# First pages split whole, and the scale bounds reduced across partitions on GpSimd, in an attention and FFN block

## The chip, the cores and the metric
The kernel runs on one core of a Trainium2 chip. The core has five engines with an instruction list each: TensorE (PE, matrix products), ScalarE (ACT), VectorE (DVE), GpSimd (POOL) and SyncE (SP, here the issuer of nearly all DMAs). Engines wait for one another through semaphores. The metric is the device time of one execution in microseconds (us), the median of several runs.

## The reference
One transformer layer on x of shape 4 x 512 x 1024, in float32:

```python
x = layernorm(x + attention(x))     # 32 query heads, 8 key/value heads of 32, rotary, causal softmax, @ wo
gate_w, up_w, down_w = gate_t * gate_s[:, None], up_t * up_s[:, None], down_t * down_s[:, None]
hidden = silu(x @ gate_w.T) * (x @ up_w.T)      # 3584 wide, weights are -1, 0 or 1 times a scale
x = layernorm(x + hidden @ down_w.T)
```

## The kernel before
All matrix operands are float16. Where one float16 is not exact enough, a tensor is kept as two parts: "hi", its rounding, made by ACT, and "lo", what is left, made by DVE. A product of two such tensors is three matmuls. The weights of the FFN are whole numbers and need one part; their scales are applied later.

The program has two stages that overlap a little. Attention goes through 16 units (8 heads of one batch each, about 46 us). For every unit PE computes projections ("proj": q, and for a new batch kv), scores by query row ("score_q", only for the row maxima that DVE takes), scores by key ("score_k"), the values times the exponentials ("pv", line 1027) and sums of the exponentials ("sums"). ACT makes the exponentials, POOL masks the diagonal block of each ("causal", line 1510), and POOL adds exponentials of two key tiles ("presum", line 1518) so that PE's sums are shorter. A projection result is rotated by DVE ("rotate", lines 1295 to 1297), added up by POOL ("rope_add", line 1504), split by ACT and DVE ("nat_hi", "nat_lo") and turned by a transposing DMA ("stack"). The FFN is a Strassen-like scheme on PE over two passes.

Nobody writes the order of instructions out. Each piece of work is `put` into a plan with an engine, a rank (a due time), a duration and the pieces that it comes after. `Plan.close` simulates the engines: of the pieces that may start, each engine takes the one with the lowest rank. The result is one list for each engine, which the hardware then executes in that order. The ranks are in slots of 46 us. A DMA's share of the queue is given as `moves`. So a changed duration, rank or dependency can reorder every engine's list.

The first twelve pages (512 KB each: x tiles, wq and wkv weights; `FIRST`, line 68) are loaded by SP at once and split in the order of loading ("split_hi" on ACT, lines 1143 and 1145; "split_lo" on DVE, lines 1271 and 1275). The first three are split in two halves (`HALVED = 3`), and PE's first products wait for half a page only.

The FFN needs a bound of the hidden values: the largest gate scale times the largest up scale, over all partitions. DVE reduces the two scale tensors (128 x 28) along the free axis, which leaves 128 x 2 numbers ("bound", 0). SP stores these to DRAM and loads all 256 of them back into every partition, in the buffer row0, and DVE reduces again (line 1403) and derives the scales that ACT's silu and DVE use in the FFN ("bound", 1). The first load of a row of x into row0 waits for it.

Of the kernel before, what the change touches and what calls it, by code (L numbers as in the profile page):

```python
# [17 lines left out]
KD = D // P  # L18
# [40 lines left out]
SLOT = 46.0  # L59
HOP = .15  # L60
LANDS = 1.9
FIRST_MOVES, PAGE_MOVES, FORM_MOVES, TURN_MOVES, FORMS_MOVE = 1.3, 1.85, .95, 1.31, 3.3
# [7 lines left out]

HALVED = 3
# [132 lines left out]
class Plan:  # L204
# [69 lines left out]
def attention_plan(plan):  # L274
# [6 lines left out]
    ranks = {w: -200.0 + n if n < NFIRST - 4 else SLOT * (-1.6 + .1 * (n - NFIRST + 4)) for n, w in enumerate(FIRST)}  # L281
# [10 lines left out]
    for n, (what, b, j) in enumerate(loads):  # L292
        at = ranks[what, b, j]
        before = n - 2 if n >= NFIRST + 2 else NFIRST - 1 if what == "wo" else -1
        last = [loads[n - 1]] if n else []
        put(SY, at, .4, "page_load", what, b, j, moves=2 * FIRST_MOVES if n == 0 else FIRST_MOVES if n < NFIRST else PAGE_MOVES,
            after=[("split_lo", *loads[before])] if before >= 0 else [])
        put(SC, at, 1.04, "split_hi", what, b, j, after=[("page_load", what, b, j)] + [("split_hi", *w) for w in last] + (
            [("proj", "q", UNITS * b - 1, j, KD - 1)] if what == "x" and b else []))
        put(VE, at, 1.25, "split_lo", what, b, j, after=[("split_hi", what, b, j)] + [("split_lo", *w) for w in last])  # L300
# [125 lines left out]
def output_done(plan, tile, end):  # L426
# [4 lines left out]
    row += [("bound", 1)] if tile == 0 else []  # L431
# [210 lines left out]
def block_kernel(nc, xT, x, wq, wkv, wo, gateT, upT, downT, gate_s, up_s, down_s,  # L642
                 rope, causal, identH, identB, out):
    bound_dram = nc.dram_tensor("scale_bounds_spill", [P, 2], F32, kind="Internal").ap()
# [8 lines left out]
    plan.put(SY, SLOT, .4, "bound_store", moves=.1, after=[("bound", 0)])  # L653
    plan.put(SY, SLOT + 3, .4, "bound_load", moves=.3, after=[("bound_store",)])
    plan.put(VE, SLOT + 6, 1.6, "bound", 1, after=[("bound_load",)])
# [5 lines left out]
    with ctx:  # L661
        def sem(name):
            return ctx.enter_context(nc.semaphore(name))
# [79 lines left out]
        s_half_hi, s_half_lo = sem("first_half_hi"), sem("first_half_lo")  # L743
# [25 lines left out]
        s_bound_out, s_bound_in = sem("bound_store_dma"), sem("bound_load_dma")  # L769
# [157 lines left out]
        def tensor_program(e):  # L927
# [12 lines left out]
            for kind, which in plan.order[PE]:  # L940
                if kind == "proj":
# [8 lines left out]
                    if what == "out":  # L950
                        if k == 0:
                            late = att_late(w)
                            on.wait_ge(s_att_in[late], 16 * len([t for t in range(w + 1) if att_late(t) == late]))
                        on.wait_ge(s_lo, split_n["wo", 0, k] + 1)
                        dst, cols = bank[n % 2][:, :], slice(part * HALF, (part + 1) * HALF)
                        left, right = att[att_late(w)], wo_p
                        rows = slice(0, P)
                    elif what == "q":
                        b, g = divmod(w, UNITS)
                        n_x, n_w = split_n["x", b, part], split_n["wq", g, k // 4]  # L960
                        if n_x < HALVED and k < KD // 2:
                            on.wait_ge(s_half_lo, n_x + 1)
                        else:
                            on.wait_ge(s_lo, n_x + 1)
                        if n_w < HALVED and k % 4 < 2:
                            on.wait_ge(s_half_lo, n_w + 1)
                        else:
                            on.wait_ge(s_lo, n_w + 1)
                        dst, cols = bank[n % 2][:, 0:UH * HD], slice(g * UH * HD, (g + 1) * UH * HD)
                        left, right = xT_p, wq_p  # L970
                    else:
                        on.wait_ge(s_lo, split_n["x", w, part] + 1)
                        on.wait_ge(s_lo, split_n["wkv", 0, k // 2] + 1)
                        dst, cols = bank[n % 2][:, :], slice(0, 2 * NKV * HD)
                        left, right = xT_p, wkv_p
# [144 lines left out]
        def scalar_program(e):  # L1120
            on = Waits(e)
            e.dma_start(tab[:, :, :, :], rope).then_inc(s_tab, 16)
            for kind, which in plan.order[SC]:
                if kind == "split_hi":
# [128 lines left out]
        def vector_program(e):  # L1253
# [7 lines left out]
            for kind, which in plan.order[VE]:  # L1261
                if kind == "split_lo":
# [4 lines left out]
                    up, whole = X_UP if which[0] == "x" else W_UP, as_parts(which[0], src)  # L1267
                    if n < HALVED:
                        mid = hi.shape[1] // 2
                        on.wait_ge(s_half_hi, n + 1)  # L1270
# [124 lines left out]
                elif kind == "bound":  # L1395
                    if which[0] == 0:
# [96 lines left out]
        def gpsimd_program(e):  # L1493
# [4 lines left out]
            for kind, which in plan.order[PO]:  # L1498
# [20 lines left out]
                elif kind == "newton":  # L1519
# [8 lines left out]
                    nc.gpsimd.tensor_scalar(w, mv[:, n % 2, 0:1], r, -1.0, ALU.mult, ALU.mult).then_inc(s_newton, 1)  # L1528
                elif kind == "scale_row":
# [41 lines left out]
        def sync_program(e):  # L1571
            on = Waits(e)
            for kind, which in plan.order[SY]:
# [42 lines left out]
                elif kind == "bound_store":  # L1616
                    on.wait_ge(s_bound, 1)
                    e.dma_start(bound_dram, sc[:, 0:2]).then_inc(s_bound_out, 16)
                elif kind == "bound_load":
                    on.wait_ge(s_bound_out, 16)  # L1620
                    e.dma_start(row[0][:, 0:2 * P], bound_dram.rearrange("a c -> (a c)").partition_broadcast(P)).then_inc(s_bound_in, 16)
# [154 lines left out]
```

## Time and profile before
| | |
|---|---|
| median of 3 runs | 1853.55 us (1852.56 to 1855.95) |
| profiled execution | 1853.55 us, its span 1851.8 us |
| PE | busy 1802.5 us, 97% of the span |
| DVE | 1188.8 us, 64% |
| ACT | 709.7 us, 38% |
| POOL | 533.6 us, 29% |

The span is the time from the first to the last instruction in the trace; the execution's own time lies a little above it. A busy share is an average over the whole span: in the first 130 us DVE is the more loaded engine beside PE, later PE is busy almost without a break. A wait of PE is put down to the instruction that released it. Instructions that load code, issue DMAs or handle semaphores do not count as busy and have no row in a timeline of busy work; they can only be seen as idle time.

### The profile page before, as it was taken

Reading aid. Unit: us, or ns where it says so; the run is one execution under the profiler, and the core shown is the slowest. Engines: PE = TensorE matmul, PEld = TensorE weight load, DVE = VectorE, ACT = ScalarE, POOL = GpSimd, SP = SyncE. Lnnn points to the kernel's source line nnn. Section 1 sums busy time; section 2 is a strip of 40 time slices with the busy share of each in tenths; the row PEclk is TensorE's granted clock in tenths of the full one; section 3 lists DMA queues with packets and bytes.
Section 4 is the critical chain, followed back from the end, with each engine's and each line's share of the span. In section 5 each row is a group of like instructions: output and inputs, shape, how many; then the busy total and the mean of one; then the engine's idle time right before and its main releaser. Section 6 shows DMA issues by size and latency. Waiting matters only on the chain.

```text
span 1851.8 us, 27052 instructions
## 1 busy us (share of the span) xinstructions
PE 1802.5 (97%) x10384; PEld 873.7 (47%) x10384; DVE 1188.8 (64%) x2063; ACT 709.7 (38%) x1115; POOL 533.6 (29%) x805
## 2 busy tenths in 40 slices
PE   8989999999999999999999999999999999999998
PEld 5645555555555533444444444444444444444444
DVE  7996778678767763555545444745656765667646
ACT  5444435344434444346433343341232322222221
POOL 2454546446546554221000000211311211122203
PEclk9999999999999998999999999999999999999999
DMA  8453334225324397567743353549311221222301
GB/s 257 103 146 55 70 92 130 60 70 144 78 49 115 92 225 214 187 223 261 249 169 131 109 196 136 213 145 211 128 66 54 73 73 42 81 95 86 118 12 80
DMA packets 228592, 233.24 MB, mean 126 GB/s; under 512 B 184048, under 2 KB 184432, under 8 KB 228464
## 3 DMA queue, kind: packets, MB, share of 16 engines
q1 hardware_dynamic: 227600, 231.13, 42.3%
q8 instruction: 82, 1.34, 0.3%
q10 hardware_dynamic: 864, 0.39, 0.1%
q14 instruction: 46, 0.38, 0.1%
HBM read 122.68 MB, written 72.88 MB: 106 GB/s over the span
## 4 chain that ended last, share of the span: by engine, by line
PE 88%; DVE 5%; issue 2%; SPq 2%; DMA 1%; ACT 1%; POOL 1%; DVEq 0%; ACTq 0%
PE bank L1082 32%; PE bank L978 21%; PE bank L1102 13%; PE bank L1115 6%; PE bank L1027 4%; PE bank L990 4%; PE bank L1014 3%; PE bank L1042 3%; PE bank L993 1%; DVE down_forms L1453 1%; SPq L1654 1%; DVE gate_blocks L1447 1%; DVE up_blocks L1437 0%; DVE down_forms L1430 0%; DVE xT_parts L1275 0%
## 5 line engine op out<-in xcount | busy, mean ns | idle before, releaser
L1082 PE MATMUL bank<-x_forms,weight_forms 128*128 128x512 f16 x3136 | 700.5, 379 | 11.7 <-DVE up_blocks L1437 3.7
L1082 PEld LDWEIGHTS bank<-x_forms,weight_forms 128*128 128x128 f16 x3136 | 305.4, 98 | 385.5 <-issue 7.1
L1174 ACT ACTIVATE p_tiles<-bank 128x512 f32<-128x512 f32 (+1 forms) x352 | 193.0, 557 | 291.9 <-PE bank L1014 290.2
L1310 DVE TENSOR_REDUCE row_max<-bank 128x1 f32<-128x384 f32 (+3 forms) x352 | 219.9, 636 | 90.8 <-PE bank L993 89.7
L1102 PE MATMUL bank<-down_forms 128*128 128x512 f16 (+1 forms) x1168 | 258.1, 376 | 2.4 <-issue 2.4
L978 PE MATMUL bank<-wq_parts,xT_parts 128*128 128x256 f16 x1536 | 216.8, 274 | 7.9 <-DVE wq_parts L1271 7.9
L1472 DVE TENSOR_TENSOR acc<-bank,acc 128x512 f32<-128x512 f32 x188 | 127.7, 687 | 123.6 <-PE bank L1102 64.7
L1510 POOL TENSOR_SCALAR_AFFINE_SELECT p_tiles<-p_tiles 128x128 f32<-128x128 f32 (+2 forms) x352 | 137.8, 398 | 219.7 <-ACT p_tiles L1174 218.4
L1102 PEld LDWEIGHTS bank<-down_forms 128*128 128x128 f16 x1168 | 114.2, 98 | 137.3 <-issue 2.9
L978 PE MATMUL bank<-wo_parts,att_parts 128*128 128x512 f16 x672 | 171.7, 384 | 1.9 <-DMA att_parts<-att_spill 1.9
L978 PEld LDWEIGHTS bank<-wq_parts,xT_parts 128*128 128x128 f16 x1536 | 144.5, 98 | 59.2 <-issue 12.5
L1534 POOL TENSOR_TENSOR acc<-acc,down_forms 128x1024 f32<-128x1024 f32 x16 | 38.8, 2429 | 375.0 <-DVE acc L1472 375.0
L1115 PE MATMUL bank<-down_forms 128*128 128x512 f16 x560 | 133.6, 379 | 1.7 <-DVE down_forms L1453 1.7
L990 PE MATMUL bank<-k_stack,q_stack 96*128 96x512 f16 (+3 forms) x512 | 126.7, 301 | 4.9 <-DVE row_max L1310 4.7
L1014 PE MATMUL bank<-q_stack,k_stack 98*128 98x512 f16 (+1 forms) x352 | 126.1, 363 | 4.4 <-ACT p_tiles L1174 2.7
L1518 POOL TENSOR_TENSOR p_tiles<-p_tiles 128x512 f32<-128x512 f32 (+1 forms) x62 | 117.2, 1890 | 42.3 <-PE bank L1027 41.8
L1437 DVE TENSOR_TENSOR up_blocks<-bank,up_blocks 128x512 f32<-128x512 f32 x84 | 58.0, 690 | 107.9 <-PE bank L1082 55.9
L1251 ACT ACTIVATE down_forms<-gate_blocks 128x512 f16<-128x512 f32 x102 | 64.0, 628 | 133.1 <-DVE gate_blocks L1447 127.1
L1437 DVE TENSOR_TENSOR gate_blocks<-bank,gate_blocks 128x512 f32<-128x512 f32 x84 | 57.7, 688 | 77.1 <-PE bank L1082 67.5
L1524 POOL TENSOR_SCALAR rstd<-rstd 128x1 f32<-128x1 f32 x93 | 35.3, 380 | 223.3 <-DVE rstd L1374 217.1
L1239 ACT ACTIVATE gate_blocks<-gate_blocks,gate_scale 128x512 f32<-128x512 f32 x84 | 60.5, 720 | 99.1 <-DVE gate_blocks L1437 99.0
L978 PEld LDWEIGHTS bank<-wo_parts,att_parts 128*128 128x128 f16 x672 | 61.6, 98 | 77.5 <-issue 17.9
(121 smaller groups left out, 2049.3 us busy)
## 6 DMA issues: line engine op xcount, KB each, us to landing
weight_forms_spill<-weight_forms SPq DMA_DIRECT2D x28, 896.0 KB, 5.3
weight_forms<-weight_forms_spill SPq DMA_DIRECT2D x28, 896.0 KB, 4.5
x_forms_spill<-x_parts SPq DMA_DIRECT2D x56, 256.0 KB, 2.3
w_page<-gateT SPq DMA_DIRECT2D x28, 512.0 KB, 5.1
w_page<-upT SPq DMA_DIRECT2D x28, 512.0 KB, 4.0
w_page<-downT SPq DMA_DIRECT2D x28, 512.0 KB, 4.1
att_spill<-att_made SPq DMA_DIRECT2D x64, 128.0 KB, 2.2
down_forms<-x_spill SPq DMA_DIRECT2D x16, 512.0 KB, 3.3
```

The costliest lines, as they stand in the source:

```text
L978: t = nc.tensor.matmul(dst, left[:, a, k, rows], right[:, c, k, cols], start=k == 0 and m == 0, stop=last)
L990: nc.tensor.matmul(to[:, h, :], qT[0:STK, u % QS, h0 + h, i * P:n], kT[0:STK, b % 2, kv_of(u, h0 + h), 0:n], start=h == 0, stop=False, ski ...
L1014: nc.tensor.matmul(to, kT[0:STKM, b % 2, (u % UNITS) * UG + G, lo:lo + P], qT[0:STKM, u % QS, heads, lo:S], start=True, stop=True).then_in ...
L1082: t = nc.tensor.matmul(strassen[bank_set(use)][to][:, :], w_form[:, use % 4, A_FORMS[a_form], k * P:(k + 1) * P], xF[:, :, B_FORMS[b_form] ...
L1102: t = nc.tensor.matmul(to[:, 0:cols.stop - cols.start], hid_p[place_of(r)][:, k, a, i // 2 * P:(i // 2 + 1) * P], wd_p[place_of(r)][:, c, ...
L1115: t = nc.tensor.matmul(to[:, :], hid_f[r % NF % 3][:, HID_FORMS.index(a_form), a, pair * P:(pair + 1) * P], wd_f[r % NF % 3][:, DOWN_B[b_f ...
L1174: nc.scalar.activation(p32[j][:, h0:h0 + heads, :], bank[5 + m % 2][:, 0:heads * n].rearrange("p (h c) -> p h c", c=n), ACT.Exp, scale=SCO ...
L1310: nc.vector.tensor_reduce(mx[:, u % 2, i, h0:h0 + ROW_HEADS[i]], bank[3 + m % 2][:, 0:ROW_HEADS[i] * n].rearrange("p (h c) -> p h c", c=n) ...
L1437: nc.vector.tensor_tensor(block, strassen[bank_set(use)]["Z" if k == 1 else "P"][:, :], block, ALU.add).then_inc(s_blk, 1)
L1472: nc.vector.tensor_tensor(dst, got[:, :], dst, ALU.add).then_inc(s_acc, 1)
L1510: nc.gpsimd.affine_select(out=block, in_=block, compare_op=ALU.is_ge, fill=0.0, base=0, pattern=[[0, KEY_HEADS[j]], [1, P]], channel_multi ...
L1518: nc.gpsimd.tensor_tensor(to, to, p32[j + 1][:, :, :], ALU.add).then_inc(s_pre, 1)
```

## The change
Three edits. The first three pages are no longer split in halves: one ACT and one DVE instruction for each page, and PE waits for whole pages. The plan's numbers for the first pages change: the last four of `FIRST` get the same early ranks as the others (before they were due 1.6 to 1.3 slots ahead of time 0), and each takes `PAGE_MOVES` of the queue. The bounds of the scales no longer go through DRAM: POOL runs a `partition_all_reduce` over 128 x 2 numbers, which leaves the maxima in every partition.

```diff
-FIRST_MOVES, PAGE_MOVES, FORM_MOVES, TURN_MOVES, FORMS_MOVE = 1.3, 1.85, .95, 1.31, 3.3
+PAGE_MOVES, FORM_MOVES, TURN_MOVES, FORMS_MOVE = 1.85, .95, 1.31, 3.3
-HALVED = 3
-    ranks = {w: -200.0 + n if n < NFIRST - 4 else SLOT * (-1.6 + .1 * (n - NFIRST + 4)) for n, w in enumerate(FIRST)}
+    ranks = {w: -200.0 + n for n, w in enumerate(FIRST)}
-        put(SY, at, .4, "page_load", what, b, j, moves=2 * FIRST_MOVES if n == 0 else FIRST_MOVES if n < NFIRST else PAGE_MOVES,
+        put(SY, at, .4, "page_load", what, b, j, moves=PAGE_MOVES,
-    row += [("bound", 1)] if tile == 0 else []
-    plan.put(SY, SLOT, .4, "bound_store", moves=.1, after=[("bound", 0)])
-    plan.put(SY, SLOT + 3, .4, "bound_load", moves=.3, after=[("bound_store",)])
-    plan.put(VE, SLOT + 6, 1.6, "bound", 1, after=[("bound_load",)])
+    plan.put(PO, SLOT, 3.0, "bound", 0, 0, after=[("bound", 0)])
+    plan.put(VE, SLOT, .8, "bound", 1, after=[("bound", 0, 0)])
...
-                        if n_x < HALVED and k < KD // 2:
-                            on.wait_ge(s_half_lo, n_x + 1)
-                        else:
-                            on.wait_ge(s_lo, n_x + 1)
...
+                        on.wait_ge(s_lo, split_n["x", b, part] + 1)
+                        on.wait_ge(s_lo, split_n["wq", g, k // 4] + 1)
...
-                    if n < HALVED:
-                        mid = hi.shape[1] // 2
-                        nc.scalar.activation(hi[:, 0:mid], whole[:, 0:mid], ACT.Copy, scale=up).then_inc(s_half_hi, 1)
...
-                        nc.vector.scalar_tensor_tensor(lo[:, 0:mid], whole[:, 0:mid], up, hi[:, 0:mid],
-                                                       ALU.mult, ALU.subtract).then_inc(s_half_lo, 1)
...
-                    on.wait_ge(s_bound_in, 16)
-                    nc.vector.tensor_reduce(sc[:, 2:4], row[0][:, 0:2 * P].rearrange("p (a c) -> p c a", c=2),
-                                            mybir.AxisListType.X, ALU.max).then_inc(s_bound, 1)
...
+                elif kind == "bound":
+                    on.wait_ge(s_set, 2)
+                    on.wait_ge(s_bound, 1)
+                    nc.gpsimd.partition_all_reduce(sc[:, 2:4], sc[:, 0:2], P, bass.bass_isa.ReduceOp.max).then_inc(s_bound, 1)
+                    on.wait_ge(s_bound, 2)
```

DVE's list at the start of the program. L1271 and L1275 are split_lo before (L1249 in the changed file), L1295 to L1297 the rotate (L1270 to L1272), L1304 nat_lo (L1279). Before:

```order
L1275 SCALAR_TENSOR_TENSOR xT_parts<-p_tiles,xT_parts 128x8x128
L1275 SCALAR_TENSOR_TENSOR wkv_parts<-p_tiles,wkv_parts 128x1024
L1295 TENSOR_TENSOR rope_cos<-bank,rope_tab 128x256
L1296 TENSOR_TENSOR rope_sin<-bank,rope_tab 128x8x16
L1297 TENSOR_TENSOR rope_sin<-bank,rope_tab 128x8x16
L1275 SCALAR_TENSOR_TENSOR wkv_parts<-wo_parts,wkv_parts 128x1024 x3
L1304 TENSOR_TENSOR stack_rows<-rope_cos,stack_rows 128x8x32
L1295 TENSOR_TENSOR rope_cos<-bank,rope_tab 128x256
```

Now:

```order
L1249 SCALAR_TENSOR_TENSOR xT_parts<-p_tiles,xT_parts 128x8x128
L1270 TENSOR_TENSOR rope_cos<-bank,rope_tab 128x256
L1271 TENSOR_TENSOR rope_sin<-bank,rope_tab 128x8x16
L1272 TENSOR_TENSOR rope_sin<-bank,rope_tab 128x8x16
L1249 SCALAR_TENSOR_TENSOR wkv_parts<-p_tiles,wkv_parts 128x1024
L1249 SCALAR_TENSOR_TENSOR wkv_parts<-wo_parts,wkv_parts 128x1024
L1279 TENSOR_TENSOR stack_rows<-rope_cos,stack_rows 128x8x32
L1270 TENSOR_TENSOR rope_cos<-bank,rope_tab 128x256
L1271 TENSOR_TENSOR rope_sin<-bank,rope_tab 128x8x16
L1272 TENSOR_TENSOR rope_sin<-bank,rope_tab 128x8x16
L1249 SCALAR_TENSOR_TENSOR wkv_parts<-wo_parts,wkv_parts 128x1024 x2
```

The first rotate has moved ahead of all four wkv pages, and nat_lo with the second rotate ahead of the last two.

POOL's list in the second group of the first unit (about 79 us in the trace). AFFINE_SELECT is causal, the TENSOR_TENSOR on p_tiles is presum, the one on rope_cos is rope_add. Before:

```order
L1510 AFFINE_SELECT p_tiles<-p_tiles 128x512
L1510 AFFINE_SELECT p_tiles<-p_tiles 128x2x128 x2
L1510 AFFINE_SELECT p_tiles<-p_tiles 128x128 x4
L1518 TENSOR_TENSOR p_tiles<-p_tiles 128x4x128
L1510 AFFINE_SELECT p_tiles<-p_tiles 128x128
L1518 TENSOR_TENSOR p_tiles<-p_tiles 128x4x256
L1504 TENSOR_TENSOR rope_cos<-rope_cos,rope_sin 128x256
L1510 AFFINE_SELECT p_tiles<-p_tiles 128x128 x3
```

Now:

```order
L1482 AFFINE_SELECT p_tiles<-p_tiles 128x512
L1482 AFFINE_SELECT p_tiles<-p_tiles 128x2x128 x2
L1504 ISA
L1504 ISA scale_bounds<-scale_bounds 128x2
L1482 AFFINE_SELECT p_tiles<-p_tiles 128x128 x5
L1490 ISA
L1490 TENSOR_TENSOR p_tiles<-p_tiles 128x4x128
L1490 TENSOR_TENSOR p_tiles<-p_tiles 128x4x256
L1476 TENSOR_TENSOR rope_cos<-rope_cos,rope_sin 128x256
L1482 AFFINE_SELECT p_tiles<-p_tiles 128x128 x3
```

The all-reduce stands behind the first three masks of the group, with an ISA instruction that has no tile ahead of it; another such instruction stands ahead of the first presum. One mask has moved ahead of that presum. Such an instruction without a tile also stands ahead of POOL's first rope_add in both kernels.

## Rows read from the trace of the kernel before

**Rows 1.** The page, the chain that ended last, shares of the span by engine.
```profile
PE 88%; DVE 5%; issue 2%; SPq 2%; DMA 1%; ACT 1%; POOL 1%; DVEq 0%; ACTq 0%
```

**Rows 2.** PE's waits, whole span: instruction, releaser, us in total, times, longest us.
```profile
PE bank L978 <- DVE wq_parts L1271: 7.9, 1, 7.9
...
PE bank L1027 <- POOL p_tiles L1510: 3.3, 3, 2.5
```

**Rows 3.** Timeline of ACT, first 10 us: start us, us, instruction, idle before and releaser.
```profile
1.23 1.28 ACT L1143 ACT_TABLE_LOAD   x1 [1.23 <-PEq L1770]
5.11 0.63 ACT L1143 ACTIVATE xT_parts<-p_tiles 128x512 f16<-128x512 f32 x1 [2.60 <-DMA p_tiles<-xT]
...
6.34 0.63 ACT L1143 ACTIVATE wq_parts<-p_tiles 128x512 f16<-128x512 f32 x1
...
8.90 1.06 ACT L1145 ACTIVATE xT_parts<-p_tiles 128x1024 f16<-128x1024 f32 x1
```

**Rows 4.** Timeline of DVE, 10 to 18 us.
```profile
10.06 1.23 DVE L1275 SCALAR_TENSOR_TENSOR xT_parts<-p_tiles,xT_parts 128x1024 f16<-128x1024 f32 x1 [0.41 <-ACT xT_parts L1145]
...
12.89 0.42 DVE L1295 TENSOR_TENSOR rope_cos<-bank,rope_tab 128x256 f32<-128x256 f32 x1 [0.33 <-PE bank L978]
...
13.62 4.02 DVE L1275 SCALAR_TENSOR_TENSOR wkv_parts<-wo_parts,wkv_parts 128x1024 f16<-128x1024 f32 x3
```

**Rows 5.** Timeline of PE, first 26 us.
```profile
7.91 7.56 PE L978 MATMUL bank<-wq_parts,xT_parts 128*128 128x256 f16 x48 [7.91 <-DVE wq_parts L1271]
15.31 10.52 PE L978 MATMUL bank<-wkv_parts,xT_parts 128*128 128x512 f16 x48
```

**Rows 6.** Timeline of POOL, 78 to 92 us.
```profile
78.67 1.54 POOL L1510 TENSOR_SCALAR_AFFINE_SELECT p_tiles<-p_tiles 128x512 f32<-128x512 f32 x3
82.06 0.68 POOL L1510 TENSOR_SCALAR_AFFINE_SELECT p_tiles<-p_tiles 128x128 f32<-128x128 f32 x2 [1.84 <-ACT p_tiles L1174]
83.77 0.67 POOL L1510 TENSOR_SCALAR_AFFINE_SELECT p_tiles<-p_tiles 128x128 f32<-128x128 f32 x2 [1.03 <-ACT p_tiles L1174]
85.65 1.54 POOL L1518 TENSOR_TENSOR p_tiles<-p_tiles 128x512 f32<-128x512 f32 x1 [1.21 <-PE bank L1027]
...
87.42 2.35 POOL L1518 TENSOR_TENSOR p_tiles<-p_tiles 128x1024 f32<-128x1024 f32 x1
89.73 0.71 POOL L1504 TENSOR_TENSOR rope_cos<-rope_cos,rope_sin 128x256 f32<-128x256 f32 x1
90.41 0.79 POOL L1510 TENSOR_SCALAR_AFFINE_SELECT p_tiles<-p_tiles 128x128 f32<-128x128 f32 x3
```

**Rows 7.** Timeline of PE, 84 to 94 us, the two values groups.
```profile
85.84 0.85 PE L1027 MATMUL bank<-p_tiles,v 128*32 128x384 f32 x8
...
92.98 1.07 PE L1027 MATMUL bank<-p_tiles,v 128*32 128x512 f32 x8
```

**Rows 8.** Timeline of POOL, its first tensor operation and the idle before it.
```profile
13.79 1.63 POOL L1504 TENSOR_TENSOR rope_cos<-rope_cos,rope_sin 128x256 f32<-128x256 f32 x1 [12.29 <-DVE rope_sin L1297]
```

**Rows 9.** DMA issues: issuing engine, operation, count, size, us from issue to landing.
```profile
row<-scale_bounds_spill SPq DMA_DIRECT2D x1, 128.0 KB, 4.8
...
scale_bounds_spill<-scale_bounds SPq DMA_DIRECT2D x1, 1.0 KB, 3.7
```

**Rows 10.** Windows: us, busy of PE, PEld, DVE, ACT, POOL, granted clock, DMA share, GB/s.
```profile
80.00:90.00 10.00, 9.92 (x93) 5.74 (x85) 9.41 (x16) 5.38 (x10) 5.74 (x9) 1.00 0.78 139
100.00:130.00 30.00, 25.42 (x225) 14.18 (x224) 27.61 (x49) 16.62 (x28) 19.61 (x26) 1.00 0.63 151
222.00:227.30 5.30, 3.47 (x21) 1.14 (x21) 4.81 (x8) 3.87 (x7) 4.78 (x8) 1.00 0.57 148
227.30:230.90 3.60, 3.58 (x11) 1.44 (x12) 1.94 (x3) 0.60 (x1) 1.12 (x3) 0.53 0.38 73
```

**Rows 11.** Timeline of PE, 110 to 131 us, the longest wait.
```profile
129.16 0.39 PE L1001 MATMUL bank<-idH,max_parts 128*16 128x128 f16 x4 [2.21 <-DVE max_parts L1320]
```

**Rows 12.** The page, costliest groups, POOL's small operation: busy us, mean ns, idle before.
```profile
L1524 POOL TENSOR_SCALAR rstd<-rstd 128x1 f32<-128x1 f32 x93 | 35.3, 380 | 223.3 <-DVE rstd L1374 217.1
```

More of the change, by code:

```diff
@@ L643, in block_kernel @@
                  rope, causal, identH, identB, out):
-    bound_dram = nc.dram_tensor("scale_bounds_spill", [P, 2], F32, kind="Internal").ap()
     x1_dram = nc.dram_tensor("x1_spill", [TILES, P, D], F32, kind="Internal").ap()
@@ L742, in block_kernel @@
         s_hi, s_lo = sem("split_hi"), sem("split_lo")
-        s_half_hi, s_half_lo = sem("first_half_hi"), sem("first_half_lo")
         s_proj, s_proj_taken, s_v = sem("projected"), sem("projection_taken"), sem("v_copied")
@@ L768, in block_kernel @@
         s_hhi, s_hlo, s_down, s_acc = sem("hid_hi"), sem("hid_lo"), sem("down"), sem("acc")
-        s_bound_out, s_bound_in = sem("bound_store_dma"), sem("bound_load_dma")
         s_bound, s_ds, s_ds_in, s_xrow, s_scaled, s_added = (
@@ L959, in tensor_program @@
                         b, g = divmod(w, UNITS)
-                        n_x, n_w = split_n["x", b, part], split_n["wq", g, k // 4]
-                        if n_x < HALVED and k < KD // 2:
-                            on.wait_ge(s_half_lo, n_x + 1)
-                        else:
-                            on.wait_ge(s_lo, n_x + 1)
[L965 to L968, printed above, removed]
+                        on.wait_ge(s_lo, split_n["x", b, part] + 1)
+                        on.wait_ge(s_lo, split_n["wq", g, k // 4] + 1)
                         dst, cols = bank[n % 2][:, 0:UH * HD], slice(g * UH * HD, (g + 1) * UH * HD)
@@ L1138, in scalar_program @@
                         on.wait_ge(s_proj, proj_n["q", which[1] * UNITS - 1, which[2]] + 1)
-                    up = X_UP if which[0] == "x" else W_UP
-                    hi, whole = parts_of(*which)[0], as_parts(which[0], src)
-                    if n < HALVED:
-                        mid = hi.shape[1] // 2
-                        nc.scalar.activation(hi[:, 0:mid], whole[:, 0:mid], ACT.Copy, scale=up).then_inc(s_half_hi, 1)
-                        hi, whole = hi[:, mid:], whole[:, mid:]
-                    nc.scalar.activation(hi, whole, ACT.Copy, scale=up).then_inc(s_hi, 1)
+                    nc.scalar.activation(parts_of(*which)[0], as_parts(which[0], src), ACT.Copy,
+                                         scale=X_UP if which[0] == "x" else W_UP).then_inc(s_hi, 1)
                 elif kind == "v_copy":
@@ L1266, in vector_program @@
                     on.wait_ge(arrived, 16 * times)
[L1267 to L1270, printed above, removed]
-                        nc.vector.scalar_tensor_tensor(lo[:, 0:mid], whole[:, 0:mid], up, hi[:, 0:mid],
-                                                       ALU.mult, ALU.subtract).then_inc(s_half_lo, 1)
-                        hi, lo, whole = hi[:, mid:], lo[:, mid:], whole[:, mid:]
                     on.wait_ge(s_hi, n + 1)
-                    nc.vector.scalar_tensor_tensor(lo, whole, up, hi, ALU.mult, ALU.subtract).then_inc(s_lo, 1)
+                    nc.vector.scalar_tensor_tensor(lo, as_parts(which[0], src), X_UP if which[0] == "x" else W_UP, hi,
+                                                   ALU.mult, ALU.subtract).then_inc(s_lo, 1)
                 elif kind == "rotate":
@@ L1615, in sync_program @@
                                 att_dram[b, t].rearrange("p a k c -> p (a k c)")).then_inc(s_att_in[att_late(tile)], 16)
[L1616 to L1621, printed above, removed]
                 elif kind == "row_load":
                     tile = which[0]
-                    if tile == 0:
-                        on.wait_ge(s_bound, 2)
                     if tile >= TILES - 2:
```

## The prediction, made before the changed kernel ran

> **What bounds the kernel now.** I read the page first, then the waits of TensorE (PE), then timelines of the stretches that the change touches. The chain that ended last lies on PE for 88% [rows 1], and PE is busy for 97% of the 1851.8 us span: what is off PE matters only where it makes PE wait. PE's waits are few: 7.9 us before its first matmul, 3.3 us in all for GpSimd's (POOL) masked tiles [rows 2]. PE executes its list in order, so one late instruction holds all behind it, and nothing later in the kernel has an idle reserve in which a delay of many microseconds could vanish. The question is what the change does to PE's waits in two places: the first 20 us, and around 80 us.
>
> The profiled execution took 1853.55 us, 1.75 us more than its span; it is also the median of the three runs, so the sum is made on it.
>
> **Part 1, the undivided first pages.** Before, x tile 0 and two wq pages are split in halves. ScalarE (ACT) begins at 5.11, when x lands, and thanks to the halves PE begins at 7.91 [rows 3, 5]. Whole pages cost 1.06 us on ACT and 1.23 us on VectorE (DVE) [rows 3, 4]. x: 5.11 + 1.06 = 6.17 on ACT, then 1.23 on DVE, 7.5 with the hand-over. wq: ACT 6.34 (its landing) + 1.06 = 7.40, DVE 7.5 + 1.22 = 8.7. PE starts at about 8.75: +0.8 us. The three instructions fewer on ACT and on DVE are already in these times.
>
> The new order changes DVE too: the first group's "rotate" moves ahead of the first wkv page, "nat_lo" and the second "rotate" ahead of the last two. The first rotate then starts at 12.89 + 0.8 = 13.7 [rows 4], though DVE was free from 11.3. Then 0.8 for the rotate, 2.5 for wkv pages 0 and 1 (17.0), 0.4 for nat_lo, 0.7 for the second rotate (18.1); wkv page 2, at 1.34 as in the run of three in 4.02 us [rows 4], is done at 19.4 to 19.8. PE begins the wkv group at 15.31 + 0.8 = 16.1 and needs page 2 after 12 of 48 matmuls, 2.6 us later (10.52 us for 48 [rows 5]), at 18.7. It waits 0.7 to 1.1 us; with the pages behind I take 1.2. The start costs +2.0 us; bounds 0.8 (only the first) and 3.
>
> **Part 2, the bounds of the scales.** Removed: a store and its broadcast load, 3.7 and 4.8 us from issue to landing [rows 9], two issues on SyncE's queue, a small reduction on DVE, and the wait of the first row load. All of this lay beside PE's work, and its result is first needed in the FFN, hundreds of microseconds later: I cost the removal at nothing; at most DVE's reduction, under half a microsecond, comes back.
>
> Added on POOL: the all-reduce and, as the order shows, an instruction without a tile just before it and one just before the next TENSOR_TENSOR. I read these two as changes of POOL's loaded code; the only other one stands, in both kernels, ahead of the first rope_add. The plan books 3.0 us for the all-reduce and nothing for the loads. The trace hides the price of the one in before: POOL sat idle 12.29 us there and was ready when DVE released it [rows 8], so it takes at most 12.29 us. From below, the nearest row is ACT's table load, 1.28 us [rows 3]. The middle is 6.8, and a small transfer out to memory and back takes 3.7 + 4.8 = 8.5 us [rows 9]. I take 7 us for each. The all-reduce of 128x2 is bounded by POOL's small operation, 0.38 us [rows 12], and by the round trip that it replaces, 8.5 us; with two elements to a partition I take 1 us, near the small row.
>
> The Trainium skill has a price for this load (GPSIMD Engine Reference, section 2.1, Instruction dispatch): the first call after a load pays about 6 us, with no visible instruction in the profile. No row here shows it. With 6 for 7, twice, the sum would be 2 us less, 1863.9; by this rule the change makes two such calls, and it speaks against the change.
>
> Now the queue. Before, POOL ends three masks at 78.67 + 1.54 = 80.21 and is idle for 1.84 us [rows 6]. There stand now the load and the all-reduce: 80.2 + 7 + 1 = 88.2. Behind them four masks (0.68 + 0.67), done at 89.4 with a hand-over less. PE's group at 85.84 [rows 7] waits for the fourth: it starts at 89.4, a stall of 3.5 us. ACT and DVE run dry with it, since their banks come from PE. On POOL one more mask (89.7), the second load (96.7), the two sums 1.54 and 2.35 (100.5), rope_add 0.71 and three masks 0.79 (102.0) [rows 6]. PE's 128x512 group, begun at 92.98 before [rows 7], needs them: it starts at 102.0. In all +9.0 us, the second stall being 5.5. Of the 15 us added to POOL, its idle takes the rest: 1.84 and 1.21 us [rows 6], 1.8 between 90.41 + 0.79 = 91.2 and 92.98, and the waits between masks.
>
> **Given back.** From 100 to 130 DVE is busy 27.6 of 30 us [rows 10], and PE waits 2.21 us for it at 129 [rows 11]. While PE stalls DVE catches up, so a part goes: I take 1.2 (bounds 0 and 3, should the smaller waits go as well).
>
> **The clock.** From 222 to 227.3 PE was busy 3.47 of 5.3 us, and in the 3.6 us after it the granted clock was 0.53, so nearly all at the lower level of 1.2 GHz [rows 10]: about 1.7 us lost. Both stalls are longer than that idle time; but from 100 to 130 single waits of up to 2.21 us left the clock at 1.00 [rows 10, 11]. I take 1.7 for the second stall, 0.8 for the first: +2.5 (bounds 0 and 5).
>
> Sum: 2.0 + 9.0 - 1.2 + 2.5 = +12.3; 1853.55 + 12.3 = 1865.9 us.
>
> **Rivals.**
> A, not slower: the loads hide. If load and all-reduce fit in the idle 1.84 us and the second load in the 3 us of 1.21 + 1.8, POOL's new work is covered, and DVE's slack around 129 pays the start's 2.0 back. It decides at a load of about 1.5 us, near the 1.28 of [rows 3]. The time is 1853.55 + 2.0 - 1.2 = 1854.4, with the start at 0.8 and 2.2 back 1852.2. Against it: every transfer from memory cited here took 3.7 us or more.
> A half way: the second load does nothing, because the code is still there. Then the first stall alone remains: 1853.55 + 2.0 + 3.5 - 1.2 + 0.8 = 1858.7.
> B, slow loads: the DMA queues move 139 GB/s from 80 to 90 us [rows 10], and a load that shares them takes 10 us to the upper bound of 12.3. Each load's excess over 7 adds to PE's delay in full: at 12.3 it is 9.0 + 5.3 + 5.3 = 19.6, the clock 3.4, and the time 1853.55 + 2.0 + 19.6 - 1.2 + 3.4 = 1877.4.
> C, a slow all-reduce, 8.5 us: +7.5, 1873.4. Past about 11 us for load and all-reduce together DVE, whose own step of the bounds waits for it, holds back row maxima too.
> For A speaks that POOL's load is invisible before; for B that the nearest row, [rows 8], would allow it; for C that nothing across partitions runs on POOL before.
>
> **How the numbers follow.** Forecast (loads of 5 to 9 us) 0.60; A 0.11; the single load 0.08; B 0.12; C 0.06; faster by a way I have not priced, DVE's catching up above all, 0.03. A difference of 0.2%, 3.7 us, is what a measurement of this kernel can tell from none. Slower: 0.60 + 0.08 + 0.12 + 0.06 less 0.01 for a single load that costs little, 0.85; the same: A and that 0.01, 0.12; faster 0.03. The forecast's own range is 1860 (loads of 5, clock at 1) to 1872 (loads of 9, clock at 5). For 8 in 10 I go down to 1857, which holds the single load, and up to 1875, which holds C and the milder half of B.
>
> **What would show it.** Right: the first matmul near 8.7 us; PE waiting about 1 us for wkv parts; on POOL a gap of about 7 us ahead of the all-reduce and again ahead of the next 128x512 sum, with no row of work in it; PE's longest waits at its values groups for POOL, 3 to 4 and 5 to 6 us; the granted clock below 1 behind the second. Wrong: PE waiting under 2 us for POOL between 80 and 110 (then the loads were mispriced, A); the gaps there but the span grown much less (given back later, to be seen in DVE's share after 100 us); no wait for wkv parts (DVE's new order was covered).

## The result, and the profile after

The changed kernel takes 1865.6 us (median of 4 runs, 1864.1 to 1866.4) beside 1853.05 us (4 runs, 1849.9 to 1856.0) for the kernel before: a ratio of 1.0067, 95% interval 1.0049 to 1.0086. It is slower, by 12.6 us; forecast were 1865.9 us. (The later comparisons timed the kernel before again, 13 to 27 runs each, with medians of 1854.1 to 1855.3 us; beside these the difference is 10.3 to 11.5 us.) The profiled execution took 1864.6 us with a span of 1862.9, 11.05 us more than that of before, and the points below are set against these 11.05 us.

The chain that ended last lies on TensorE (PE) for 87% (88% in [rows 1]): PE is still the bound. PE's waits, over the whole span (instruction, releaser, us in total, times, longest), answer to [rows 2]:
```profile
PE bank L964 <- DVE wq_parts L1249: 8.9, 1, 8.9
PE bank L1013 <- POOL p_tiles L1482: 8.3, 4, 2.7
...
PE bank L964 <- DVE wkv_parts L1249: 0.9, 2, 0.7
```
The first matmul comes 1.0 us later, there is a new wait for wkv parts, and the waits for GpSimd (POOL) went from 3.3 to 8.3 us. PE's start, beside [rows 5]:
```profile
8.87 7.04 PE L964 MATMUL bank<-wq_parts,xT_parts 128*128 128x256 f16 x48 [8.87 <-DVE wq_parts L1249]
15.74 2.75 PE L964 MATMUL bank<-wkv_parts,xT_parts 128*128 128x512 f16 x12
19.19 1.47 PE L964 MATMUL bank<-wkv_parts,xT_parts 128*128 128x512 f16 x6 [0.70 <-DVE wkv_parts L1249]
```
VectorE (DVE) at the same time, beside [rows 4]: the first rotate's product stands ahead of every wkv page, after 1.95 us of idle time, and the next rotate ahead of the last two pages.
```profile
10.15 1.22 DVE L1249 SCALAR_TENSOR_TENSOR xT_parts<-p_tiles,xT_parts 128x1024 f16<-128x1024 f32 x1
13.32 0.42 DVE L1270 TENSOR_TENSOR rope_cos<-bank,rope_tab 128x256 f32<-128x256 f32 x1 [1.95 <-PE bank L964]
...
17.93 2.88 DVE L1249 SCALAR_TENSOR_TENSOR wkv_parts<-wo_parts,wkv_parts 128x1024 f16<-128x1024 f32 x2
```
POOL's timeline from 78 us, beside [rows 6]. Both gaps are "issue": POOL waited for nothing that the profile shows. The instructions without a tile have no row here, but the view of a line lists them, as MODIFY_POOL_CONFIG (POOL's configuration instruction): at 83.0 us ahead of the all-reduce and at 91.6 us ahead of the sum. Each gap begins there.
```profile
80.53 2.53 POOL L1482 TENSOR_SCALAR_AFFINE_SELECT p_tiles<-p_tiles 128x512 f32<-128x512 f32 x3
89.77 0.48 POOL L1504 PARTITION_ALL_REDUCE scale_bounds<-scale_bounds  x1 [6.71 <-issue]
90.33 1.28 POOL L1482 TENSOR_SCALAR_AFFINE_SELECT p_tiles<-p_tiles 128x128 f32<-128x128 f32 x5
98.31 3.74 POOL L1490 TENSOR_TENSOR p_tiles<-p_tiles 128x512 f32<-128x512 f32 x2 [6.70 <-issue]
102.01 0.72 POOL L1476 TENSOR_TENSOR rope_cos<-rope_cos,rope_sin 128x256 f32<-128x256 f32 x1
102.68 0.79 POOL L1482 TENSOR_SCALAR_AFFINE_SELECT p_tiles<-p_tiles 128x128 f32<-128x128 f32 x3
```
PE's two values groups, beside [rows 7]; they began at 85.84 and 92.98 before. These two waits are 5.4 of the 8.3 us:
```profile
91.42 1.50 PE L1013 MATMUL bank<-p_tiles,v 128*32 128x384 f32 x8 [2.73 <-POOL p_tiles L1482]
...
103.53 1.11 PE L1013 MATMUL bank<-p_tiles,v 128*32 128x512 f32 x8 [2.69 <-POOL p_tiles L1482]
```
Windows, with columns as in [rows 10]; the granted clock is the third number from the end:
```profile
90.80:97.60 6.80, 6.18 (x29) 2.95 (x30) 2.29 (x7) 1.79 (x3) 0.81 (x4) 0.50 0.20 42
97.60:104.30 6.70, 4.01 (x37) 2.65 (x39) 2.56 (x5) 0.63 (x1) 5.02 (x6) 1.00 0.02 4
104.40:107.80 3.40, 3.40 (x22) 0.82 (x15) 2.20 (x10) 0.00 (x0) 0.72 (x1) 0.50 0.40 77
...
1797.00:1801.00 4.00, 3.16 (x8) 1.15 (x9) 0.69 (x1) 0.02 (x1) 0.00 (x0) 0.57 0.00 0
```
The clock stood at its lower level (1.2 GHz, 0.50 of full) behind each of the two stalls. Near 1797 us it fell once more, which it did not in the same window of the kernel before:
```profile
1797.00:1801.00 4.00, 4.00 (x21) 1.78 (x19) 3.10 (x7) 0.00 (x0) 2.27 (x6) 1.00 0.00 0
```

Both kernels have 10,384 matmuls. Counting them in the order of their starts and taking one trace from the other gives PE's delay at any time of before. It is what the steps below are measured by: 2.8 us at 78 us; 5.6 at the first values group and 10.55 at the second; 10.1 from 154 to 1200 us; 9.6 at 1340; 11.05 at 1840. How far chance goes in it the launches with the same first pages show, at 78 us: -0.3, -0.4, 0.6 and 0.0 us with those of before (e1, e5, e6, e9), 2.8, 2.8 and 4.0 us with those of the change (the changed kernel, e2, e3).

### The profile page after: what moved, and what is told of

Read it like the earlier page. It is cut to its first block, busy times and chain, and to the rows that moved or that the text cites. A ratio compares the mean times of both kernels' runs of the same rounds, so it can differ in the third digit from the quotient of the medians.

```text
span 1862.9 us, 27050 instructions
## 1 busy us (share of the span) xinstructions
PE 1808.5 (97%) x10384; PEld 875.0 (47%) x10384; DVE 1187.1 (64%) x2059; ACT 709.8 (38%) x1112; POOL 529.4 (28%) x806
## 4 chain that ended last, share of the span: by engine, by line
PE 87%; DVE 6%; issue 2%; SPq 2%; DMA 1%; POOL 1%; ACT 1%; DVEq 0%; ACTq 0%; POOLq 0%
PE bank L1068 32%; PE bank L964 20%; PE bank L1088 13%; PE bank L1101 6%; PE bank L1013 4%; PE bank L976 3%; PE bank L1000 3%; PE bank L1028 2%; PE bank L979 1%; DVE down_forms L1425 1%; SPq L1623 1%; DVE gate_blocks L1419 1%; DVE row_max L1285 0%; DVE up_blocks L1409 0%; DVE down_forms L1402 0%
## 5 line engine op out<-in xcount | busy, mean ns | idle before, releaser
L1068 PE MATMUL bank<-x_forms,weight_forms 128*128 128x512 f16 x3136 | 700.4, 379 | 11.1 <-DVE up_blocks L1409 3.7
L1013 PE MATMUL bank<-p_tiles,v 128*32 128x128 f32 (+3 forms) x1024 | 95.0, 451 | 8.4 <-POOL p_tiles L1482 8.3
L964 PE MATMUL bank<-wkv_parts,xT_parts 128*128 128x512 f16 x384 | 97.8, 379 | 0.9 <-DVE wkv_parts L1249 0.9
```

The costliest lines, as they stand in the source:

```text
L964: t = nc.tensor.matmul(dst, left[:, a, k, rows], right[:, c, k, cols], start=k == 0 and m == 0, stop=last)
L1013: t = nc.tensor.matmul(bank[PV_BANK[q]][h * HD:(h + 1) * HD, lo:S], value, p32[j][:, h, :], start=j == NT - 1, stop=j == 0, tile_position= ...
L1068: t = nc.tensor.matmul(strassen[bank_set(use)][to][:, :], w_form[:, use % 4, A_FORMS[a_form], k * P:(k + 1) * P], xF[:, :, B_FORMS[b_form] ...
```

## The experiments

The times of before in these comparisons are medians of 1854 to 1855 us (13 to 27 runs). One launch's trace carries chance of its own: stretches at the low clock near 227 and 1790 us come and go between launches and those near 700 us vary in length, a shorter one being worth about 1.7 us. So the ratios decide between kernels, and the traces show places.

**e1: the all-reduce alone.** The kernel before in all its orders and pages; only the bounds go through POOL.
```diff
+    plan.order[SY] = [p for p in plan.order[SY] if p[0] not in ("bound_store", "bound_load")]
+    plan.order[PO].insert(plan.order[PO].index(("causal", (0, 1, 2, 2))) + 1, ("bound", (0, 0)))
```


> The kernel before, with its own lists on every engine, in which alone the DRAM round trip of the bounds is taken out and the all-reduce stands on POOL behind the third mask of the second group. My theory: two gaps of 6.7 us on POOL, PE 3 us late behind the first and 8.1 us late behind the second, of which DVE's slack gives back at most 2; with about 1.5 us for a lower clock the time is 1853 + 8 = 1860 to 1862 us. Rival (the reordering of the lists is the larger part of the +11 us): 1853 to 1856.

Measured: 1863.97 us, ratio 1.0047 (1.0032 to 1.0062). POOL, and what PE waited for from 78 to 130 us:
```profile
85.46 0.55 POOL L1529 PARTITION_ALL_REDUCE scale_bounds<-scale_bounds  x1 [5.54 <-ACT p_tiles L1174]
86.08 1.05 POOL L1507 TENSOR_SCALAR_AFFINE_SELECT p_tiles<-p_tiles 128x128 f32<-128x128 f32 x4
93.92 1.25 POOL L1515 TENSOR_TENSOR p_tiles<-p_tiles 128x512 f32<-128x512 f32 x1 [6.80 <-issue]
```
```profile
PE bank L1027 <- POOL p_tiles L1507: 7.5, 3, 5.6
```
PE's delay goes from -0.3 us at 78 to 8.3 at 111. Most of the loss is here, with the start untouched. The view puts the first gap, 5.54 us, down to ACT's exponentials; but the all-reduce reads only scale_bounds, and its MODIFY_POOL_CONFIG stands at 79.9 us, where the gap begins. I take it for the load, shorter than the 6.71 us above. The time lies above the 1860 to 1862 us that I had expected; the trace has two low-clock stretches that its kernel before has not, near 138 and 1797 us.

**e2: the start alone.** Whole pages and the new ranks, the bounds by the round trip.
```diff
-HALVED = 3
+HALVED = 0
-    ranks = {w: ... else SLOT * (-1.6 + .1 * (n - NFIRST + 4)) ...}
+    ranks = {w: ... else -200.0 + n ...}
-        put(SY, at, .4, "page_load", ..., moves=2 * FIRST_MOVES if n == 0 else ...,
+        put(SY, at, .4, "page_load", ..., moves=PAGE_MOVES,
```


> The changed kernel's first pages and plan numbers alone; the bounds go through DRAM as before. My theory: the first matmul near 8.8 us, PE 2.7 to 2.9 us late from 35 to 95 us, and about 1 us late from 180 us on, since DVE's slack gives the rest back: 1853 + 1 = 1854 us, within noise. Rival (the start's delay stays to the end): 1856.

Measured: 1853.99 us, ratio 0.9995 (0.9984 to 1.0007). PE is 2.8 us late at 78 us and 0.5 at 154: the start's delay is given back almost whole.

**e3: a second all-reduce behind the first**, in the changed kernel. It tells the price of the operation from the price of what stands ahead of it.
```diff
+                    nc.gpsimd.partition_all_reduce(sc[:, 6:8], sc[:, 0:2], P, ...ReduceOp.max)
```


> The changed kernel with a second all-reduce of the same numbers directly behind the first, into two unused columns. My theory (the 6.7 us ahead of the all-reduce is the change of POOL's code): the second begins without such a gap, costs 0.5 us, and the time is 1865 to 1867 us. Rival (the gap is the launch of an all-reduce): another gap of 6.7 us, and the time is 1871 to 1873 us.

Measured: 1866.5 us (one run). POOL:
```profile
90.92 0.54 POOL L1505 PARTITION_ALL_REDUCE scale_bounds<-scale_bounds  x1 [6.64 <-issue]
91.57 0.35 POOL L1507 PARTITION_ALL_REDUCE scale_bounds<-scale_bounds  x1
92.00 1.28 POOL L1483 TENSOR_SCALAR_AFFINE_SELECT p_tiles<-p_tiles 128x128 f32<-128x128 f32 x5
100.76 3.73 POOL L1491 TENSOR_TENSOR p_tiles<-p_tiles 128x512 f32<-128x512 f32 x2 [7.48 <-issue]
```
The second one costs 0.35 us and has no gap. The gap belongs to the exchange of POOL's code, not to the all-reduce. The five masked selects run straight behind an all-reduce; the way back is paid by the next TENSOR_TENSOR.

**e4: the all-reduce first on POOL.** The scales are loaded first and DVE forms their maximum first; the hope was that POOL's 12.3 idle us [rows 8] hide everything.
```diff
+    plan.order[PO].insert(0, ("bound", (0, 0)))
+    plan.order[VE].insert(0, ("bound", (0,)))
```


> As the first kernel, but the scales are loaded at the start of the program, DVE reduces them first, and POOL's all-reduce stands ahead of its first rope_add, where POOL was idle for 12.29 us. My theory: the loads of code fall into that idle, the first rope_add comes 1 to 2 us later at 15.4, PE does not notice, and the time is that of before, 1852 to 1854 us. Rival (the loads cost PE their time wherever they stand, or the loads collide with the first pages): 1858 or more.

Measured: 1862.47 us, ratio 1.0038 (1.0023 to 1.0053). My expectation was wrong and the rival right:
```profile
12.74 0.69 POOL L1530 PARTITION_ALL_REDUCE scale_bounds<-scale_bounds  x1 [11.25 <-issue]
23.57 0.71 POOL L1502 TENSOR_TENSOR rope_cos<-rope_cos,rope_sin 128x256 f32<-128x256 f32 x1 [10.14 <-issue]
```
```profile
PE bank L980 <- DVE rope_sin L1298: 5.0, 1, 5.0
```
```profile
2.00:12.00 10.00, 3.70 (x18) 2.61 (x19) 5.13 (x10) 6.84 (x9) 0.00 (x0) 1.00 0.99 383
13.00:23.00 10.00, 8.24 (x51) 4.81 (x49) 4.42 (x7) 2.28 (x3) 0.43 (x1) 1.00 0.84 336
23.00:30.00 7.00, 3.75 (x9) 1.34 (x10) 4.60 (x8) 5.69 (x8) 2.35 (x2) 0.53 0.27 54
```
DVE had the maxima only at 6.35 us, 6.4 us before the all-reduce, and its MODIFY_POOL_CONFIG stands at 1.7 us, ahead of the wait for them. If the load ran from there it took 11.0 us, if only once the maxima were ready, 6.4 us; no run tells which. The second gap is 10.14 us, and the rotate that it held up had been ready for 9.3 us, so this load took 9.3 to 10.1 us. This load ran while DMA moved 336 GB/s. The rope sum came at 23.57 instead of 13.79, DVE and then PE waited, and the clock fell.

**e5: the all-reduce where POOL is idle.** Before, POOL has nothing to do from 229.5 to 242.45 us, and DMA moves nothing from 230 to 240 us.
```diff
+    plan.order[PO].insert(plan.order[PO].index(("causal", (4, 1, 2, 2))) + 1, ("bound", (0, 0)))
+    plan.order[VE].remove(("bound", (1,)))
+    plan.order[VE].insert(plan.order[VE].index(("row_max", (5, 3, 5))) + 1, ("bound", (1,)))
```


> The kernel before, with the DRAM round trip replaced by the all-reduce, placed on POOL in the 12.9 us that POOL is idle from 229.5 us on (before its masked select of unit 4 at 242.45), and DVE's second step of the bounds behind it in the idle 1.7 us at 243. No DMA transfer runs from 230 to 240 us in the kernel before. Theory (the cost is what POOL's loads put in front of PE, and a load takes 6.7 us when DMA is quiet): load 6.7 + all-reduce 0.5 + load 6.7 = 13.9 us, ends at 243.4, 1 us after the next select was due; PE at most 1 us later: 1852 to 1856 us, ratio 0.999 to 1.001. Rival (the code load costs wherever it stands, or takes 10 us or more, as it did at the start): 20 us from 229.5, PE stalls 6 us or more: 1860 to 1865. A second rival, that leaving out the round trip brings something in itself: below 1850.

Measured: 1860.88 us, ratio 1.0041 (1.0028 to 1.0055). The theory's number was wrong. POOL, one window, and PE's next values group:
```profile
234.93 0.37 POOL L1531 PARTITION_ALL_REDUCE scale_bounds<-scale_bounds  x1 [5.92 <-issue]
240.87 0.29 POOL L1509 TENSOR_SCALAR_AFFINE_SELECT p_tiles<-p_tiles 128x128 f32<-128x128 f32 x1 [5.57 <-ACT p_tiles L1176]
248.40 1.25 POOL L1517 TENSOR_TENSOR p_tiles<-p_tiles 128x512 f32<-128x512 f32 x1 [7.23 <-issue]
```
```profile
230.00:240.00 10.00, 10.00 (x67) 3.85 (x65) 4.51 (x8) 0.63 (x1) 0.37 (x1) 1.00 0.00 0
```
```profile
250.45 1.51 PE L1029 MATMUL bank<-p_tiles,v 128*32 128x384 f32 x8 [3.23 <-POOL p_tiles L1509]
```
The first load was hidden. The second did not begin in the 5.57 us that POOL then spent idle: the next instruction in its queue was a masked select, which needs no load and waited for ScalarE (ACT). Only behind it came the TENSOR_TENSOR (line 1517) with its MODIFY_POOL_CONFIG at 241.2 us, and the load, 7.23 us, fell into POOL's busy time:
```profile
L1517 POOLq MODIFY_POOL_CONFIG  x2: 11/11/11, 241.2 to 241.2; - x2
```
So what counts would be when the load is called for, not how long POOL idles; e9 tests it.

**e6: twenty-four loads that nobody waits for.** e5, and in POOL's idle stretch of the FFN twelve all-reduces, each followed by a small TENSOR_SCALAR.
```diff
+    at = plan.order[PO].index(("x1_form", (7, "T4"))) + 1
+    plan.order[PO][at:at] = [("probe", (i,)) for i in range(12)]
```


> The kernel of e5 with twelve more pairs on POOL (an all-reduce of the same 128x2 and a small tensor_scalar on its result, nobody reads it) in POOL's idle stretch from 867 to 1149 us, where DMA moves about 190 to 260 GB/s. 24 more code loads. Theory: nobody waits for them, so the time is that of e5 within 0.1%; and if DMA traffic lengthens a load, those that meet 260 GB/s and more take longer than the 6.7 us of a quiet stretch, up to 9 or so, within one kernel and with no other engine late. Rival 1 (a load took 10 to 11 us at the start only because it was the first, cold): all 24 take 6.5 to 7.5 us whatever DMA does. Rival 2 (loads disturb the transfers of others): the kernel is over 5 us slower than e5 though nobody waits for POOL.

Measured: 1860.76 us, against 1860.88 for e5: 24 loads, some 170 us of POOL's time, cost nothing that can be measured. PE's distance to e5's trace is the same, 5.6 us, at 870 and at 1060 us. The idle time before the twelve all-reduces, that before the twelve TENSOR_SCALARs, and the window:
```profile
  issue: 78.4, 12
```
```profile
  issue: 91.3, 12
```
```profile
875.00:1060.00 185.00, 185.00 (x859) 83.79 (x857) 93.00 (x159) 75.43 (x103) 8.89 (x24) 1.00 0.53 182
```
A load ahead of an all-reduce took 6.53 us on the mean, the one back 7.61 us. PE was busy for all of the 185 us. The gaps spread from 5.83 to 8.80 us ahead of the all-reduce and from 6.71 to 9.96 us on the way back, so my rival 1 (all 6.5 to 7.5 us) falls. But DMA traffic alone does not set them, as I had thought it might. Two loads ahead of an all-reduce, and the windows of their gaps (the last number is GB/s):
```profile
899.25 0.37 POOL L1536 PARTITION_ALL_REDUCE scale_bounds<-scale_bounds  x1 [8.80 <-issue]
943.69 0.63 POOL L1536 PARTITION_ALL_REDUCE scale_bounds<-scale_bounds  x1 [5.85 <-issue]
```
```profile
890.44:899.25 8.81, 8.81 (x42) 4.02 (x41) 7.58 (x13) 3.37 (x4) 0.01 (x2) 1.00 0.98 329
937.84:943.69 5.85, 5.85 (x29) 2.65 (x27) 2.48 (x5) 2.70 (x4) 0.00 (x1) 1.00 0.81 304
```
On the way back the longest, 9.96 us, had 154 GB/s beside it, and 7.29 us went with 361 GB/s. Over the twelve loads of each way the correlation with the traffic is 0.58 and 0.29.

**e7 and e8: the two halves of the start.** e7 has whole pages and the old order, e8 the halves and the new order.

> The kernel before with HALVED = 0 alone: the first three pages are not divided, every engine's order stays. Theory: the first matmul comes 0.8 to 1.0 us later and everything behind it by the same, until DVE's slack after 100 us takes it back: 1853 to 1855. Rival (the divided pages hide no more than the launch, ACT and DVE catch up by 20 us): no delay left at 25 us.

> The kernel before with the new ranks and move times alone (the page halves stay): DVE's first rotate ahead of its first wkv page, as in the change. Theory: the first matmul stays at 7.9, PE waits 1.5 to 2 us for wkv parts behind 15 us, and is 1.7 us late at 78 us; given back by 165: 1852 to 1855. Rival (the order alone costs nothing because DVE waits for ACT and DMA anyway): under 0.5 us at 78.

Measured: e7 1856.1 us, one run; PE starts at 8.89 us and is 1.6 us late at 20 and at 78 us, where I had expected 0.8 to 1.0. e8 1848.4 us, one run; PE's waits in the first 30 us are
```profile
PE bank L978 <- DVE wq_parts L1271: 8.0, 1, 8.0
PE bank L978 <- DVE wkv_parts L1275: 0.9, 2, 0.7
```
and it is 1.1 us late at 78 us; I had expected a wait of 1.5 to 2 us and 1.7 us late. 1.6 and 1.1 together are the 2.8 us of e2 but for 0.1, which is closer than one launch can tell: e10, the kernel of e8 again, was 2.6 us late at 50 us, where e8 was 0.8. The wait for wkv parts belongs to the new order, with or without whole pages. The 1848 us looked like a gain, so the same kernel was timed again as e10.

**e9: both loads inside the idle stretch.** e5 with the first product of the bounds on POOL instead of DVE. It is useful work, and it calls for the standard code at once.
```diff
                     on.wait_ge(s_bound, 2)
+                    nc.gpsimd.tensor_scalar(sc[:, 4:5], sc[:, 2:3], sc[:, 3:4], HID_BOUND, ALU.mult, ALU.mult).then_inc(s_bound, 1)
```


> e5 with one thing more: the first product of the bounds (128x1) goes from DVE to POOL, right behind the all-reduce. In e5 POOL's select at 240.87 needed no load, and the second load (7.23 us) began only at 241.2, when the next TENSOR_TENSOR came up; behind the all-reduce the product now calls for it at 235.4, inside POOL's idle stretch. Theory (what counts is when the second load is called for): 5.9 + 0.4 + 6.7 to 7.2 + 0.3 ends at 242.5 to 243.0, the select due at 242.45 is 0.5 us late at most, PE's wait of 3.2 us for POOL at 250 goes, and the clock's low record there with it: 1852 to 1856 us, ratio 0.999 to 1.001, 5 to 7 us faster than e5. Rival (it is the exchange of code or the missing round trip that costs 6 us, not the place): 1859 to 1862 like e5.

Measured: 1855.24 us beside 1855.3 of before, ratio 0.9994 (0.9983 to 1.0006). POOL:
```profile
235.08 0.37 POOL L1529 PARTITION_ALL_REDUCE scale_bounds<-scale_bounds  x1 [5.50 <-issue]
242.45 0.25 POOL L1531 TENSOR_SCALAR scale_bounds<-scale_bounds 128x1 f32<-128x1 f32 x1 [7.00 <-issue]
242.67 0.28 POOL L1507 TENSOR_SCALAR_AFFINE_SELECT p_tiles<-p_tiles 128x128 f32<-128x128 f32 x1
242.94 1.26 POOL L1515 TENSOR_TENSOR p_tiles<-p_tiles 128x512 f32<-128x512 f32 x1
```
The MODIFY_POOL_CONFIG of the way back stands 6 us earlier than in e5:
```profile
L1531 POOLq MODIFY_POOL_CONFIG  x2: 83/83/83, 235.4 to 235.4; - x2
```
PE has no wait at all between 230 and 300 us, and its clock from 250.2 to 253.6 is 1.00 where e5 had 0.50. Same all-reduce, same two loads, same place; one instruction calls for the second load 6 us earlier, and the loss of 0.4% is gone. Nor is anything gained: with its loads covered, the all-reduce is no faster than the round trip through DRAM that it replaces, which had cost PE nothing that can be measured.

**e10 and e11.** e10 is e8's kernel timed more often; e11 has e9's bounds and e10's order.

> The kernel of e8 again, timed in five rounds. e8's one run took 1848.4 us, with PE 1.1 us late at 78 us, 2.8 early from 235 us and 5.2 early from 700. Theory (its two low-clock records fewer at 227 and 691 are the gain, and whether they fall so is chance from run to run): 1851 to 1855, ratio 0.998 to 1.001. Rival (the order alone is faster): 1847 to 1850, ratio 0.996 to 0.998.

> e9 and the new order of e10 together: the candidate for a kernel that beats both. If e9 costs nothing and the order brings what its first run showed: 1848 to 1851, ratio 0.997 to 0.998. If the first run of the order was chance: 1852 to 1856.

Measured: e10 1853.85 us (11 runs, 1850.3 to 1858.5), ratio 0.9991 (0.9982 to 1.0000). e8's single run was a low draw. The two profiled executions of this one kernel have spans of 1846.6 and 1856.7 us; e10's has the lower clock near 68, 1352 and 1792 us, e8's does not. These windows are e8's and then e10's:
```profile
60.00:80.00 20.00, 18.59 (x156) 10.92 (x158) 17.92 (x39) 9.86 (x18) 11.04 (x18) 1.00 0.41 81
...
1340.00:1360.00 20.00, 17.32 (x82) 7.67 (x80) 8.24 (x12) 7.99 (x13) 1.64 (x1) 1.00 0.21 78
```
```profile
60.00:80.00 20.00, 18.59 (x145) 11.21 (x144) 17.00 (x38) 7.17 (x14) 7.38 (x13) 0.91 0.39 82
...
1340.00:1360.00 20.00, 17.32 (x74) 7.27 (x73) 11.98 (x14) 7.43 (x12) 5.77 (x4) 0.91 0.14 47
```
e11 took 1853.31 us, ratio 0.9988 (0.9980 to 0.9997): 0.8% below the changed kernel, and below the one before by a margin that its interval just separates from none; at 2 us, and among several kernels tried, I would not build on it.

## Why the prediction was right

**The forecast's two causes hold.** The start alone is worth nothing in the end (e2, 0.9995), the all-reduce alone 1.0047 (e1), and once its loads are covered 0.9994 (e9). The rivals fall: A (loads hidden), since PE waited 5.4 us for POOL between 80 and 110 us, where A allowed under 2; the single load, since both gaps are there; B and C by the gaps of 6.7 us and the operation of 0.48.

**Start, +2.0 forecast, 2.8 measured.** The first matmul at 8.75 came at 8.87. The wait for wkv parts was where I put it, 0.90 us for 0.7 to 1.1. PE was 1.7 us late at 20 us and 2.5 at 35; I had followed DVE's new order only up to 20 us. But kernels with the same first pages lie up to 1.2 us apart at 78 us, so the 0.8 us more than forecast may be chance.

**POOL's queue, +9.0 forecast, 7.8 measured** (10.55 less 2.8). First stall: 5.6 less 2.8 is 2.8, forecast 3.5; second: 5.0, forecast 5.5. The waits themselves are not what I had named as signs, 3 to 4 and 5 to 6 us: they are 2.73 and 2.69. Of the second delay's 5.0 us, PE lost 2.2 beforehand, running at the lower clock between the two groups. From the end of the three masks at 83.0 to PE's group at 103.53 are 20.5 us, where I had 80.2 to 102.0, 21.8: the loads took 6.71 and 6.70 instead of 7, the all-reduce 0.48 instead of 1. The 6 us that the Trainium skill states for the first call after a load (GPSIMD Engine Reference, section 2.1, Instruction dispatch) are nearer to e9's quiet 5.50 than to the 6.7 here. Its rule that such a load shows no instruction agrees with the trace: no row of work stands in either gap.

**Given back, -1.2 forecast, 2.6 measured.** Behind the second stall the delay is 10.55 and 1.7 of clock, together 12.25; from 154 us it is 10.1, another 0.5 go before 1340 us. That DVE's load gives part of a delay back is what e2 shows too, where 2.3 of 2.8 us went between 78 and 154 us. With the start untouched (e1) only some 0.8 us went: 8.3 us at 111 and 1.7 for the low clock near 138 are 10.0, and 9.25 were left at 154. So what is given back is for the most part the start's delay. It was within the bounds (0 and 3), at their far end.

**The clock, +2.5 forecast, 3.1 measured, but not at the two places I named.** Behind the second stall it was the forecast 1.7 (3.4 us at 0.50, PE busy throughout). Behind the first, for which I had 0.8, it stood low for 6.8 us and cost nothing beyond the queue's delay: PE was slower there, but had to wait for POOL in the end anyway, 2.69 us. In its place stand 1.45 us near 1797, which I count as chance: of the kernels with the all-reduce some have this low stretch (the changed one, e1, e3, e5, e9) and some lack it (e4, e6, e11), and so do those without (e7 and e10; before, e2 and e8). That the change makes it no likelier is not shown.

Together 2.8 + 7.8 - 2.6 + 3.1 = 11.1 of the 11.05 us. The mechanism was right, but that +12.3 came so near has luck in it: the start and the clock came out higher than forecast (0.8 and 0.6 us), POOL's queue and what is left after the giving back lower (1.2 and 1.4 us), and 1.45 us of the clock's term are the chance stretch near 1797.

**What I got wrong afterwards.** Twice I expected the all-reduce to vanish in an idle stretch. In e4 I took the loads' 6.7 us for a constant and the maxima for ready. In e5 I added the two loads as if they followed each other; they don't, unless something calls for the second. e5's trace shows 4.8 us lost at the place, its runs 6.8 us: the other 2 us are not explained by a row, and the low-clock stretches near 1352 and 1793 us, where the trace of before has none, may be no more than chance.

## What to carry to other kernels

Here an operation of another code library on POOL cost two loads, most of them 5.5 to 8 us long and a few up to 10, and the operation itself (0.35 to 0.69 us) hardly counted. Ask first whether what it replaces is on the bounding engine's path at all; here the round trip was not. If it must be used, put it where POOL is idle for both, and put an instruction of the standard code right behind it, so that the way back starts at once and not when the next one is due. A single run or a single trace does not tell 0.5% here: the same kernel gave spans 10 us apart.

## What the runs showed of the hardware

- A code load on POOL took 5.50 to 6.71 us ahead of an all-reduce (the changed kernel, e1, e3, e5, e9, e11) and 6.70 to 7.54 us on the way back; in e6 5.83 to 8.80 and 6.71 to 9.96 us, 6.53 and 7.61 on the mean; in e4 one took 9.3 to 10.1 us at 336 GB/s. That traffic lengthens it is not shown: in e6 loads at 329 and 304 GB/s took 8.80 and 5.85 us, and the changed kernel's took 6.71 and 6.70 us at 195 and 23 GB/s.
- The masked select ran behind an all-reduce without a load, TENSOR_TENSOR and TENSOR_SCALAR did not (the changed kernel, e3, e5, e6).
- A repeated all-reduce of 128x2 took 0.35 us and needed no second load (e3).
- Twenty-four loads in 185 us in which PE was busy throughout cost PE nothing (e6).
- A MODIFY_POOL_CONFIG stood in POOL's queue ahead of each operation that paid a load, and the gap began with it: behind a select that waited for ACT at 241.2 us (e5), right behind the all-reduce at 235.4 us (e9).
